# One decoder layer on one core: query rows ordered by element then head, groups 0 and 1 copied on chip, items reordered in the prologue

## The reference

```python
def bitnet_linear(x, weight, scale_param):
    s = jnp.maximum(jnp.mean(jnp.abs(weight), axis=1), 1e-08)
    y = jnp.einsum('bsi,oi->bso', x, jnp.sign(weight / s[:, None]))
    return jnp.nan_to_num(y * (s * scale_param)[None, None, :], ...)
x = x + attention(layernorm(x))       # 32 query heads, 8 key/value heads, HEAD_DIM 16
x = x + ffn(layernorm(x))             # silu(x W1) * (x W3) @ W2, W = base + mean|w-base| * sign(w-base)
```

## Time and profile before

| | us |
|---|---|
| median of 3 runs | 1011.42 (1007.2 to 1011.43) |
| the profiled execution | 1005.97 |
| its span | 1004.2 |
| PE busy | 951.8 (95%) |
| DVE, ACT, POOL busy | 711.0, 553.3, 298.4 |
| PE's share of the chain that ended last | 80% |

### The profile page before, as it was taken

How to read it: one execution, slowest core, us unless ns; L and a number is a source line. 1 busy time by engine, 2 the same in 40 slices (tenths; PEclk the granted TensorE clock), 3 DMA queues, 4 the chain that set the end, 5 groups by cost and what they waited for, 6 DMA issues and landing times.

```text
span 1004.2 us, 14700 instructions
## 1 busy us (share of the span) xinstructions
PE 951.8 (95%) x4962; PEld 617.7 (62%) x4962; DVE 711.0 (71%) x950; ACT 553.3 (55%) x1078; POOL 298.4 (30%) x306
## 2 busy tenths in 40 slices
PE   6699999999999999978899999999999999999997
PEld 5344433443444333333668888888888888888886
DVE  5688898889887889866864578655886558854443
ACT  5468889889988989846852322333224232232221
POOL 4755467448644613444011101011010111101110
PEclk9689999999999999988999999999999999999999
DMA  5736667567646677612840002310023100220001
GB/s 190 192 92 184 173 178 203 146 196 196 192 121 180 187 204 237 181 43 86 272 164 31 1 1 83 112 62 0 0 84 121 51 0 0 84 85 0 0 0 42
DMA packets 77700, 109.74 MB, mean 109 GB/s; under 512 B 6736, under 2 KB 30288, under 8 KB 77648
## 3 DMA queue, kind: packets, MB, share of 16 engines
q1 hardware_dynamic: 76912, 108.23, 36.1%
q10 hardware_dynamic: 416, 0.66, 0.2%
q0 software_dynamic: 320, 0.20, 0.1%
HBM read 75.17 MB, written 32.77 MB: 107 GB/s over the span
## 4 chain that ended last, share of the span: by engine, by line
PE 80%; DVE 5%; ACT 5%; DMA 4%; SPq 3%; issue 2%; POOL 1%; DVEq 0%; ACTq 0%; POOLq 0%
PE psum L1603 15%; PE psum L1604 15%; PE psum L1605 15%; PE psum L1504 9%; PE psum L1494 8%; PE psum L1478 5%; PE psum L1407 2%; ACT probs L986 2%; DVE nmx L1157 2%; PE psum L1593 2%; PE psum L1515 2%; PE psum L1408 2%; PE psum L1516 2%; DMA k_slot<-k_stack 1%; DMA q_slot<-shift 1%
## 5 line engine op out<-in xcount | busy, mean ns | idle before, releaser
L1157 DVE TENSOR_REDUCE nmx<-psum 128x2 f32<-128x1024 f32 x256 | 305.2, 1221 | 63.3 <-PE psum L1478 61.0
L986 ACT ACTIVATE probs<-psum 128x512 f32<-128x512 f32 x512 | 271.1, 603 | 48.6 <-PE psum L1494 47.0
L846 POOL CAST dh<-w2T 128x512 fp32r<-128x512 f32 (+1 forms) x56 | 50.8, 908 | 432.0 <-PE psum L1605 393.7
L1603 PE MATMUL psum<-fxh,wh 128*128 128x512 f32 x448 | 175.4, 391 | 2.2 <-DVE wl L1330 2.2
L1604 PE MATMUL psum<-fxl,wh 128*128 128x512 f32 x448 | 175.2, 391 | 0.0
L1605 PE MATMUL psum<-fxh,wl 128*128 128x512 f32 x448 | 174.9, 390 | 0.0
L1494 PE MATMUL psum<-q_slot,k_slot 50*128 50x512 f32 x512 | 149.3, 471 | 18.8 <-ACT probs L986 8.6
L1494 PEld LDWEIGHTS psum<-q_slot,k_slot 50*128 50x128 f32 x512 | 64.4, 186 | 134.8 <-ACT probs L986 62.4
L1504 PE MATMUL psum<-probs,v_slot 128*32 128x512 f32 x1024 | 139.0, 615 | 0.0
L1337 DVE TENSOR_TENSOR gate<-gate,psum 128x512 f32<-128x512 f32 x56 | 38.4, 686 | 133.9 <-PE psum L1605 131.6
L1044 ACT ACTIVATE hh<-gate 128x512 fp32r<-128x512 f32 x56 | 35.4, 632 | 162.0 <-DVE gate L1337 162.0
(11 more groups left out here) (133 smaller groups left out, 1318.4 us busy)
## 6 DMA issues: line engine op xcount, KB each, us to landing
stage<-in_L_ffn_mean_w_dram SPq DMA_DIRECT2D x84, 256.0 KB, 4.5
q_slot<-q_stack SPq DMA_DIRECT2D x62, 192.0 KB, 3.4
stage<-in_L_ffn_w_dram SPq DMA_DIRECT2D x42, 256.0 KB, 5.4
q_stack<-q_hi SPq DMA_DIRECT2D x32, 256.0 KB
weighted_values<-u_sb SPq DMA_DIRECT2D x32, 256.0 KB, 3.9
k_slot<-k_stack SPq DMA_DIRECT2D x62, 96.0 KB, 3.6
q_stack<-q_lo SPq DMA_DIRECT2D x16, 256.0 KB
an<-weighted_values SPq DMA_DIRECT2D x16, 256.0 KB
```

Source lines behind the costliest of these rows:

```text
L846: nc.gpsimd.tensor_copy(dh[parity][:], w2T[:, bass.ds(src, 1), :].rearrange("p o c -> p (o c)")).then_inc(dh_ok, 1)
L986: nc.scalar.activation(probs[kt][:, j, :], BANK[ring_bank(("score", g, kt, j))], ACT.Exp, scale=HEAD_DIM ** -0.5).then_inc(exp_ok, 1)
L1157: v.tensor_reduce(column, pair, AX.X, ALU.max, negate=True).then_inc(s_max, 1)
L1603: mm(o, lhs_hi, rhs_hi, start=first, stop=False)
```

## The change

Query weight rows are loaded in another order, so that a query item holds its rows by half (two heads of a group), then element, then head, and `q_stack` has the shape [groups, 2, 48, 2, 512] in place of [groups, 4, 48, 512]. A load of a group's queries then reads 48 runs of 1024 elements; a store of a query item writes 4 pieces of 32 rows in place of 8 pieces of 16. The weight comes with 16 DMAs of 32 rows in place of two DMAs, and the scales of the three later query tiles and of the output projection with seven DMAs on SP in place of POOL's.

Groups 0 and 1 are both filled on chip: `first_heads` and `first_keys` take the group, SP issues 14 such DMAs and POOL 10, ACT none. The load of group 1 from DRAM goes. SP then stores the keys and query item 1, loads group 2, and only then issues the first six weight-difference DMAs and the first shift; before, these six stood ahead of the load of group 1. The query item 0 of the first element is no longer stored.

The items are now keys, queries 0, queries 1, values, queries 2, 3, in all batch elements, with `VT_AT` three slices later. In the prologue the values' item is projected before the scores, and items 4 and 5 are cut in halves of two matmul pairs (four matmuls), which stand after score steps 2, 3, 10 and 11. The warm-up is 64 transposes in place of 40.

```diff
-ITEMS = (KTILE, QT, VTILE, QT + 1, QT + 2, QT + 3)
+ITEMS = (KTILE, QT, QT + 1, VTILE, QT + 2, QT + 3)
-VT_AT = 16
+VT_AT = 19
-SELECT_AT = (6, 11)
+SELECT_AT = (0, 4, 8)
+ITEM_PIECES = {2: (4, 0), 3: (4, 1), 10: (5, 0), 11: (5, 1)}
-    q_dram = nc.dram_tensor("q_stack", [GROUPS, REP, ROWS, SEQ], FP32, kind="Internal").ap()
+    q_dram = nc.dram_tensor("q_stack", [GROUPS, 2, ROWS, 2, SEQ], FP32, kind="Internal").ap()
-    WARM = 40
+    WARM = 64
     def first_heads(...):
-            eng.dma_start(q_slot[0][r:r + HEAD_DIM, jj, :].bitcast(FP32),
-                          src[HEAD_DIM * (2 * h + jj):HEAD_DIM * (2 * h + jj + 1)].bitcast(FP32)).then_inc(done, 16)
+            eng.dma_start(q_slot[g][r:r + HEAD_DIM].bitcast(FP32), src[HALF * g + 32 * h:HALF * g + 32 * (h + 1)].bitcast(FP32)
+                          ).then_inc(done, 16)
     def load_group(eng, g, s, done):
-                          q_dram[g, 2 * h:2 * h + 2].rearrange("j r t -> r j t")).then_inc(done, 16)
+                          q_dram[g, h]).then_inc(done, 16)
     def store_item / place(r):
-                return q_dram[g:g + 2, :, r:r + HEAD_DIM, :].rearrange("g j d t -> (g j) d t")
+                return q_dram[g:g + 2, :, r:r + HEAD_DIM, :, :].rearrange("g h d j t -> (g h) (d j) t")
     SP, prologue:
-        sp.dma_start(w_nat[:, QT, :], q_w[0:P, :]).then_inc(w_in[1], 16)
-        sp.dma_start(w_nat[:, QT + 1:QT + 4, :], q_w.rearrange("(t p) c -> p t c", p=P)[:, 1:, :]).then_inc(w_in[2], 16)
+        for t in range(KT):
+            for h in range(4):
+                rows = slice(t * P + 32 * h, t * P + 32 * (h + 1))
+                sp.dma_start(w_nat[32 * h:32 * (h + 1), QT + t, :], q_w[rows, :].rearrange("(j d) c -> d j c", j=2)
+                             ).then_inc(w_in[1 if t == 0 else 2], 16)
...
     PE, prologue:
-            if nn == 2:
-                pe.wait_ge(signs_ok, OT)
-                first_item(3)
+            if nn in ITEM_PIECES:
+                first_item_piece(*ITEM_PIECES[nn])
-            if nn == 6:
-                first_item(4)
-            if nn == 12:
-                first_item(5)
```

More of the change, by code:

```diff
@@ L207, in decoder_layer @@
     scl_in = sem("scl_in")
+    scl_more = sem("scl_more")
     const_ok = sem("const_ok")
@@ L477, in _ @@
         sp.wait_ge(qh_ok, 1)
-        first_keys(sp, 1, slot_in[0])
-        first_keys(sp, 2, slot_in[0])
+        first_keys(sp, 0, 1, slot_in[0])
         sp.wait_ge(qh_ok, 2)
         for part in range(2):
-            first_heads(sp, part, 0, slot_in[0])
+            first_heads(sp, 0, part, slot_in[0])
+        for part in range(2):
+            first_heads(sp, 1, part, slot_in[1])
+        for part in (1, 2):
+            first_keys(sp, 1, part, slot_in[1])
         store_item(0, 0)
-        store_item(0, 1)
+        store_item(0, 2)
+        group_stored(2)
+        load_group(sp, 2, 2, slot_in[2])
         load_difference(0, 0)
         load_difference(0, 1)
-        group_stored(1)
-        load_group(sp, 1, 1, slot_in[1])
-        store_item(0, 2)
         def load_shift(g, s):
@@ L673, in _, with load_scale @@
         pool.wait_ge(const_ok, 5)
-        for src, t0, tiles in ((k_s, KTILE, 1), (q_s, QT, 4), (v_s, VTILE, 1), (o_s, OT, 4)):
-            nc.gpsimd.dma_start(scl[:, t0:t0 + tiles], src.rearrange("(t p) -> p t", p=P),
-                                allow_slow_non_contiguous=True).then_inc(scl_in, 16)
+        def load_scale(dst, src, done):
+            nc.gpsimd.dma_start(dst, src, allow_slow_non_contiguous=True).then_inc(done, 16)
+        load_scale(scl[:, KTILE:KTILE + 1], k_s.rearrange("(t p) -> p t", p=P), scl_in)
+        for j in range(2):
+            load_scale(scl[j:P:2, QT:QT + 1], query_scale(0, j), scl_in)
+        load_scale(scl[:, VTILE:VTILE + 1], v_s.rearrange("(t p) -> p t", p=P), scl_in)
         def token_factor(b):
@@ L699, in norm_tokens @@
             if t == 0:
-                token_factor(b)
+                if b > 1:
+                    token_factor(b)
                 pool.wait_ge(rstd_ok, b + 1)
@@ L732, in split_item @@
             pool.wait_ge(yg_ok, n + 1)
-            if c >= Q_RING:
-                pool.wait_ge(part_out[c % Q_RING], STORES * (c // Q_RING))
             if Q_RING <= c < Q_RING + 2:
-                pool.wait_ge(slot_in[0], FIRST_LOADS)
-                pool.wait_ge(first_in, FIRST_POOL)
+                for g in range(2):
+                    pool.wait_ge(slot_in[g], FIRST_SP[g])
+                    pool.wait_ge(first_in[g], FIRST_POOL[g])
+            if c >= Q_RING and c != Q_RING + 1:
+                pool.wait_ge(part_out[c % Q_RING], store_count(c - Q_RING))
             nc.gpsimd.tensor_copy(q_hi[c % Q_RING][:], g_alt[n % 2][:]).then_inc(qh_ok, 1)
@@ L906, in _ @@
             magnitude(m)
-        act.wait_ge(w_in[1], 16)
+        act.wait_ge(w_in[1], 64)
         magnitude(QT)
@@ L1397, in transpose_tokens, with project_item @@
             last.then_inc(xT_ok, 1)
-        def project_item(b, i, bank, half=None, first=False):
+        def project_item(b, i, bank, half=None, first=False, pieces=(0, KT)):
             m = ITEMS[i]
@@ L1403, in project_item @@
             c = slice(0, SEQ) if half is None else slice(HSEQ * half, HSEQ * (half + 1))
-            for kt in range(KT):
+            for kt in range(*pieces):
                 if first:
@@ L1408, in project_item @@
                 last = mm(BANK[bank][:, c], signs[:, kt, w], xl[:, kt, c], start=False, stop=(kt == KT - 1))
-            last.then_inc(q0_mm if half == 0 else q_mm, 1)
+            if pieces[1] == KT:
+                last.then_inc(q0_mm if half == 0 else q_mm, 1)
         def transpose_values_in(b, bank):
@@ L1422, in first_item, with first_item_piece @@
             project_item(0, i, 4 + i % 2)
+        def first_item_piece(i, h):
+            if h == 0:
+                positive(pe, yq_ok, i - 1)
+            project_item(0, i, 4 + i % 2, pieces=(KT // 2 * h, KT // 2 * (h + 1)))
         for _ in range(WARM):
@@ L1436, in _ @@
         first_item(1)
+        transpose_signs(QT + 1)
+        pe.wait_ge(signs_ok, 4)
         first_item(2)
-        for m in (QT + 1, QT + 2, QT + 3):
-            transpose_signs(m)
+        transpose_signs(QT + 2)
+        transpose_signs(QT + 3)
+        first_item(3)
+        pe.wait_ge(signs_ok, OT)
         def output_factors():
```

104 lines of the change are left out of this document (54 added, 50 removed).

## The result

The changed kernel is slower: 1026.97 us median (1026.06 to 1038.09, 4 runs), the kernel before, run beside it, 1010.52. So it is slower, by some 16 to 26 us. Forecast were 1047 and slower. The sign and the cause came out as written; the size did not, by 20 us.

What follows compares the result with a forecast made beforehand. TensorE, busy 95%, bounds the kernel; the query stores' DMA engines decide the change. 1005.97 (profiled execution) - 2.7 (prologue) + 43.7 (slices: 39.7 + 3 + 1) = 1047 us, range 1010 to 1068.

Steps and rivals of the forecast that it cites:

- Four engines: Query stores: four pieces use four engines at 21 GB/s each, 4.7 us more per query item on those engines.
- By bytes the storing eight do 66%, 90 of 136 engine-us, 11.3 us each: Groups with a query store: the eight storing engines are already busy for 89% of the 12.7 us period.
- each run of four: Slices: three runs of four query stores, 16.0 us per group, 64 us per run, +44.9 us together.
- the slack of 5.2: Slices: 2.6 us of backlog cost nothing in each of the second and third runs of query stores.
- +3: Slices: loads of groups 8, 16 and 24 wait for a query item stored one group earlier, +3 us in all.
- +1: Slices: of element 0's query stores in groups 0 and 1, the first fits and the second costs about +1 us.
- -2.7: Prologue: slice 0 begins at 56.5 in place of 59.2 us, -2.7 us, between -6 and +1.
- rival 2: Slices: four engines, but the backlog mostly fits, 13.5 us per store group; 1016, up to 1030 us; chance 0.15.
- Warm-up -1.5: Prologue: 64 warm-up transposes may keep the clock up, so token transposes end 1.5 us earlier, between 0 and -2.
- 53 to 56: Prologue: by TensorE alone, slice 0 would begin at 53 to 56 us.
- rival 4: Prologue gains nothing, the first shift landing at 60 us: 3 us on top of any case; no separate chance given.
- The stall: Prologue, score step 8: the 4.08 us idle before group 1's scores goes whole; the first shift is late next.

Runs made afterwards that it cites:

- run 5: Kernel before with query stores of two outermost pieces (2x64x512) in place of eight: 1139.46 us, ratio 1.1321.
- run 2: Kernel before with key and query stores of 128 outermost rows: 996.62 us, ratio 0.9892.
- Run 4: Changed kernel with the prologue's six weight DMAs behind the first shift: 1025.79 us; the same move with stores of 64 or more outermost rows: 1000.29 us.
- run 1: Kernel before with only the query stores narrowed, to four outermost pieces in place of eight: 1031.52 us, ratio 1.0242.
- run 6: Changed kernel with the shifts of groups 1 to 31 issued by ScalarE: 1052.49 us; the same move with 16-engine stores: 1006.96 us.

## Why the prediction was right in sign and too high in size

- **Four engines: right.** The share is 0.24 to 0.26, and the load of group 2 (48.9, forecast 46 to 48) and the shifts show each link behind it. The rate per engine was 25 GB/s, not 21; a query item alone thus costs four engines 7.9 us (196.6 kB / 25). Eight need 3.9 at that rate and 4.7 at the 21 of the earlier trace rows, so the term is +3.1 to +3.9 and not +4.7.
- **The failed step: "By bytes the storing eight do 66%, 90 of 136 engine-us, 11.3 us each".** It took the busy share of an engine for used capacity and fixed its rate at 17.7 GB/s. The four engines moved 21 to 22 GB/s in the changed kernel's runs, two moved 24.3 in run 5, and run 2 shows that the share hardly depends on who carries the bytes: 0.64 with all 16 engines loaded alike, 0.67 with eight. So a busy engine in a mixed stretch still had room; why it counts as busy is not shown. A group with a store took 13.8 us on average, not 16.0: 11.3 falls to 9.9 (13.8 less 3.9).
- **The sum over the three runs.** Forecast were 64 us for each run of four, +44.9; measured 55.9, 54.3 and 55.4, +18.4. With 13.8 in place of 16.0 the same working gives 55.2 each, +18.5; that is no test, since 13.8 is these three runs' own mean. With the slack of 5.2 off, +3, +1 and -2.7 it is 1020.6. The profiled 1027.6 is 7 above: the slack did not show (the runs lose 6 us each, the second and third too, 5.2), the prologue gave nothing (3.0), groups 0 and 1 lost 2.1 in place of 1, and behind the attention there are 2.1 of the kind that differs between executions. The other way the +3 for waiting loads is no term beside the runs, outside of which 1.3 us were won. All this is near rival 2, whose 1016 to 1030 hold what was measured; its 13.5 us per group are close to 13.8. The argument against it was the 89% busy, the step that failed.
- **The prologue: wrong, in three places.** Warm-up -1.5 came as -1.4 at the transposes and was eaten at the scores, where the 64 KB copies (4.79 us) made PE wait 1.85 us: they began at 31.11, forecast 29. I had counted the copies' issues and not their transfers. By TensorE alone slice 0 could have begun at about 57, not at 53 to 56: the score steps end at 56.87, and the granted clock is 0.50 from 34 us on. The first shift was issued as written (54.39, forecast 53 to 54.5) but landed at 59.4, not by 58; it took 4.41 us behind six weight transfers. Slice 0 at 59.56 was rival 4's 60. Run 4 shows the six weight DMAs by themselves, -3.2 us, and that the slices would have taken it back.
- **The stall goes, and what is late next was named rightly**: score step 8 has no wait, the first shift took its place.
- **The signs named in advance.** The share and score step 8 came as written, group 2's load a microsecond late. The periods of the first run are 12.8, 15.6, 12.3 and 15.1 us where 15 to 17 were named, TensorE waited for shifts 12.2 us in place of 40, and SP's three weight DMAs took 3.8 us in place of over 5: all three forecast too dear, as the step above would have it.
- **The pace of the runs.** The engines, not the items' order, set it: run 1, with the old order, loses 16.5 us there, and a head start of 3 us is worth nothing (run 4).

The version that beats both is the kernel before with stores of 128 outermost rows: 996.62 us, 0.9892 of before; with the longer warm-up it is the same. The on-chip copies of group 1 and the new item order add nothing to it that could be measured.

## What to carry to other kernels

Look at the slowest dimension of every DMA on both sides before its bytes: the same 256 KB were moved by 16, 8, 4 or 2 engines here, by how the DRAM tensor is laid out, and a layout made for longer runs on the load side narrowed the store. Interleaving the stacked parts made both sides wide at no cost that could be measured. And do not divide bytes by the busy share of DMA engines to find how full they are; double or halve the load and read the period.

## What the runs showed of the hardware

- Stores of 256 KB moved 383 GB/s with 128 outermost rows (run 2), 166 with 8, 101 with 4 (changed kernel), 51 with 2 (run 5): 21 to 25.5 GB/s for each engine used, by shares of 0.99, 0.52, 0.26 and 0.13. The number of engines, the largest up to 16 that divides the slowest dimension of both sides, is a rule of the Trainium skill, in "DMA: Bandwidth & Descriptors", "Why a DMA increments its semaphore by 16 and not by 1"; the traces agree at all four counts.
- A transfer of 8 KB on another engine's queue took 5.4 to 7.0 us just behind query stores on four engines (run 6), as long as on the queue of the stores (4.8 to 6.9).
- The clock in the prologue does not follow from TensorE's own program: with 40 warm-up transposes it was at 0.50 during the token transposes in the profiles of the kernel before and of run 1, and at 1.00 in that of run 2, whose matmuls are the same in number and order. The mean granted clock of the kernel before also went from 0.964 to 0.983 between executions, with times of 1012.95 and 1000.6 us.
